# Counts multiplied without stride, tile numbers rounded in floating point, weight halves made ahead of the one-hot loop and in the waits behind it

## The reference

```
xn = layernorm(x)                                   # 4096 tokens of 256
scores = softmax(xn @ gate_w.T + gate_b)            # 8 experts
top_w, top_i = top_k(scores, 2)
y = sum over the two experts: top_w * ((silu(xn @ w1.T + b1) * (xn @ w3.T + b3)) @ w2.T + b2)
z = (silu(xn @ ws1.T + bs1) * (xn @ ws3.T + bs3)) @ ws2.T + bs2
out = x + time_mix(xn) + y + z
```

## Time and profile before

| what | value |
|---|---|
| median of 3 runs | 474.6 (473.55 to 476.1) |
| profiled execution: its own time | 473.8 |
| profiled execution: span from first to last instruction | 472.0 |
| mean granted clock of TensorE | 0.985 of full speed |
| busy: TensorE / VectorE / ScalarE / GpSimd | 440.8 (93%) / 365.9 (78%) / 241.6 (51%) / 230.3 (49%) |
| chain that ended last: TensorE / VectorE / GpSimd / ScalarE | 64% / 14% / 9% / 4% |

### The profile page before, as it was taken

The page is one execution under the profiler, slowest core; times in us unless marked ns, Lnnn a source line. Parts: engine busy times, 40 slices in busy tenths (PEclk is TensorE's granted clock), DMA queues, the critical chain, the costliest instruction groups (busy, mean ns, idle before and its releaser), DMA issues.

```text
span 472.0 us, 8323 instructions
## 1 busy us (share of the span) xinstructions
PE 440.8 (93%) x2534; PEld 370.8 (79%) x2534; DVE 365.9 (78%) x684; ACT 241.6 (51%) x396; POOL 230.3 (49%) x224
## 2 busy tenths in 40 slices
PE   0998687979999999999999899999999999999997
PEld 0562455858888888888888778798888989898987
DVE  5976968968787887878766689995968787877863
ACT  4777734678668595966765532333324132324131
POOL 3333747434858666488854377651433415160000
PEclk9999679999999999999999999999999999999999
DMA  7999923245764865443473773826153443431001
GB/s 228 341 305 395 228 69 101 80 178 190 253 215 146 264 184 167 135 134 117 123 208 109 288 273 97 274 63 214 56 165 115 126 152 123 156 113 67 24 24 44
DMA packets 45858, 77.24 MB, mean 164 GB/s; under 512 B 5908, under 2 KB 32252, under 8 KB 45820
## 3 DMA queue, kind: packets, MB, share of 16 engines
q1 hardware_dynamic: 37580, 55.87, 34.1%
q0 software_dynamic: 8240, 20.88, 17.0%
HBM read 48.52 MB, written 28.21 MB: 163 GB/s over the span
## 4 chain that ended last, share of the span: by engine, by line
PE 64%; DVE 14%; POOL 9%; issue 7%; ACT 4%; DMA 1%; SPq 0%; DVEq 0%; POOLq 0%; ACTq 0%
PE ps_g L1109 11%; PE ps_y L1109 6%; PE ps_w L1569 5%; PE ps_w L1571 5%; PE ps_w L1570 5%; PE ps_w L1635 5%; PE ps_w L1636 5%; PE ps_w L1634 5%; POOL xg L1032 4%; PE ps_G L619 3%; PE ps_x L1103 2%; PE ps_h L1129 2%; PE ps_T L605 2%; PE ps_v L1570 1%; PE ps_r L1571 1%
## 5 line engine op out<-in xcount | busy, mean ns | idle before, releaser
L1032 POOL DMA_INDIRECT xg<-xn_rows,tile_tok x71 | 71.4, 1005 | 26.7 <-issue 18.6
L1545 POOL DMA_INDIRECT yg<-expert_rows,rows x64 | 67.9, 1061 | 23.6 <-issue 17.1
L1109 PE MATMUL ps_g<-w_hi,x_hi 128*128 x142 | 56.2, 396 | 2.2 <-DVE x_lo L1264 2.2
L1109 PE MATMUL ps_g<-w_lo,x_hi 128*128 x142 | 56.3, 396 | 0.0
L1109 PE MATMUL ps_g<-w_hi,x_lo 128*128 x142 | 56.1, 395 | 0.0
L1676 ACT ACTIVATE sact<-ps_w,vec_b 128x512 f32<-128x512 f32 x32 | 22.0, 687 | 58.4 <-PE ps_w L1571 58.4
L1569 PE MATMUL ps_w<-col_hi,s_hi 128*128 128x512 f32 x128 | 50.5, 395 | 0.4 <-DVE shid L1787 0.4
L1570 PE MATMUL ps_w<-col_lo,s_hi 128*128 128x512 f32 x128 | 50.2, 392 | 0.0
L1571 PE MATMUL ps_w<-col_hi,s_lo 128*128 128x512 f32 x128 | 50.2, 392 | 0.0
L1109 PE MATMUL ps_y<-w_hi,h_hi 128*128 x142 | 43.2, 304 | 1.3 <-DVE h_lo L1280 1.3
L1273 DVE TENSOR_TENSOR hid<-ps_g,act 128x512 f32<-128x512 f32 (+1 forms) x36 | 23.7, 659 | 24.4 <-ACT act L1185 24.4
(11 more groups left out here) (255 smaller groups left out, 1276.9 us busy)
## 6 DMA issues: line engine op xcount, KB each, us to landing
expert_rows<-y SPq DMA_DIRECT2D x35, 256.0 KB, 2.2
w_lo<-w_all SPq DMA_DIRECT2D x16, 384.0 KB, 9.9
table<-mix_tables SPq DMA_DIRECT2D x8, 768.0 KB, 6.2
xn_rows<-xn SPq DMA_DIRECT2D x16, 256.0 KB, 8.1
xn_columns<-xT SPq DMA_DIRECT2D x8, 512.0 KB
col<-xn_columns SPq DMA_DIRECT2D x8, 512.0 KB, 5.0
res<-x SPq DMA_DIRECT2D x16, 256.0 KB, 2.9
out<-res SPq DMA_DIRECT2D x16, 256.0 KB, 2.2
```

The costliest lines, as they stand in the source:

```text
L1032: pool.indirect_dma_start(out=xg[b][:, t, :], out_offset=None, in_=xn_d[:, :], in_offset=bass.IndirectOffsetOnAxis(ap=tile_tok[:, first_ti ...
L1109: mm = nc.tensor.matmul(out, x[:, k, :], w[:, ds(e, 1), k, cols].rearrange("p o n -> p (o n)"), start=(k == 0 and n == 0), stop=(last and ...
L1545: pool.indirect_dma_start(out=yg[a.buf(2)][:, k, q, :], out_offset=None, in_=y_d[:, :], in_offset=bass.IndirectOffsetOnAxis(ap=picked[a.bu ...
```

## The change

The counts: `hot` is read as it lies (token block, expert), and the order by expert is made where the result is written into `ps_cnt`. The tile numbers: instead of adding 127, converting to int32, shifting by 7 and converting back, a large constant (128 times 2 to the 23rd) is added and subtracted again in fp32, which rounds to a multiple of 128; `ntile`, `last` and `start` are then in rows and not in tiles, so the product with 128 becomes a sum, and `last_b` is divided by 128 and made behind `start`. ScalarE makes all of `made_hi` and `made_lo` for pieces 0 to 3 before its exponentials, and rounds all 16 pieces before `terms`. TensorE does `rest(2)` and `rest(3)` ahead of the one-hot loop, and loads the registers of the first two duos before `turn_x(0)`. VectorE halves pieces 0 to 3 between `gates` and `terms`, 4 to 7 behind `terms`, and 8 to 11 two by two later.

```
-        MADE, BOTH, HIGH, LOW = 4, 6, 13, 2
+        MADE, BOTH, HIGH, LOW = 4, 6, 16, 8
...
+        WHOLE = float(P << 23)
...
-            for i in range(2):
+            for i in range(MADE):
                 made_hi(act, i)
+            for i in range(MADE):
+                made_lo(act, i)
             nc.scalar.activation(early[:, 0:1], gb[:], ACT.Exp)
             exps(0, 0, EARLY)
             exps(1, EARLY, NSTEP)
...
-            for i in range(2, MADE):
-                made_hi(act, i)
-            for i in range(2):
-                made_lo(act, i)
             act.wait_ge(s_xn, NSTEP)
             act.wait_ge(s_xna, NSTEP)
             for i in range(MADE, HIGH):
                 split(i)
-            for i in range(2, MADE):
-                made_lo(act, i)
             act.wait_ge(s_terms, 3)
...
-                    mm = nc.tensor.matmul(ps_cnt[:, h, :].rearrange("p (e j) -> p e j", e=E), sums[:],
-                                          hot[:, k].rearrange("p j e -> p e j"), start=(k == 0), stop=(k == TOPK - 1))
+                    mm = nc.tensor.matmul(ps_cnt[:, h, :].rearrange("p (e j) -> p j e", e=E), sums[:], hot[:, k],
+                                          start=(k == 0), stop=(k == TOPK - 1))
             mm.then_inc(s_cnt, 1)
             for i in range(FIRST, MADE):
                 less(i)
-            for i in range(FIRST):
+            for i in range(MADE):
                 rest(pe, i)
...
-            for i in range(FIRST, BOTH):
+            for i in range(MADE, BOTH):
                 rest(pe, i)
...
-            own.link(nc.vector.tensor_scalar(ntile_i[:], filled[:, :, NT - 1], float(P - 1), float(P), ALU.add,
-                                             ALU.max))
-            own.link(nc.vector.tensor_scalar(ntile_i[:], ntile_i[:], 7, None, ALU.arith_shift_right))
-            own.link(nc.vector.tensor_copy(ntile[:], ntile_i[:]))
+            own.link(nc.vector.tensor_scalar(ntile[:], filled[:, :, NT - 1], (P - 1) / 2, WHOLE, ALU.add, ALU.add))
+            own.link(nc.vector.tensor_scalar(ntile[:], ntile[:], WHOLE, float(P), ALU.subtract, ALU.max))
             own.link(nc.vector.tensor_tensor_scan(out=last[:], data0=ones_f[:, 0:E], data1=ntile[:],
                                                   initial=0.0, op0=ALU.mult, op1=ALU.add))
-            nc.vector.tensor_copy(last_b[:], last[:])
             own.link(nc.vector.tensor_tensor(start[:], last[:], ntile[:], ALU.subtract))
-            own.link(nc.vector.scalar_tensor_tensor(out=place, in0=start[:, None, :].broadcast_to([P, NT, E]),
-                                                    scalar=float(P), in1=place, op0=ALU.mult, op1=ALU.add))
+            nc.vector.tensor_scalar(last_b[:], last[:], 1.0 / P, None, ALU.mult)
+            own.link(nc.vector.tensor_tensor(place, place, start[:, None, :].broadcast_to([P, NT, E]), ALU.add))
...
             nc.vector.tensor_tensor(gates[:, 1, :], gates[:, 1, :], gates[:, 0, :], ALU.mult)
+            for i in range(4):
+                split_lo(dve, i)
             dve.wait_ge(s_terms, 4)
...
-            for i in range(LOW):
+            for i in range(4, LOW):
                 split_lo(dve, i)
...
-            es = {}
             pe.wait_ge(s_tok, 1)
+            es = {a: experts(a) for a in range(2)}
             turn_x(0)
...
-            for i in range(HIGH, E * KC):
-                split_hi(act, i)
             cut_x(2)
...
-            for i in range(LOW, 5):
-                split_lo(dve, i)
             cut_x(0)
-            for i in range(5, 8):
+            for i in range(8, 10):
                 split_lo(dve, i)
             hidden(0)
             cut_x(1)
-            for i in range(8, 12):
+            for i in range(10, 12):
                 split_lo(dve, i)
```

More of the change, by code:

```diff
@@ L298, in route @@
         eps_t = sb("eps_t", [P, 1], F32)
-        ntile_i = sb("ntile_i", [P, E], I32)
+        WHOLE = float(P << 23)
         ntile = sb("ntile", [P, E], F32)
@@ L806, in vector @@
                                                   data0=keep[:].rearrange("p e j -> p (e j)"),
-                                                  data1=ps_cnt[:, 1, :], initial=0.0,
-                                                  op0=ALU.mult, op1=ALU.add))
+                                                  data1=ps_cnt[:, 1, :], initial=0.0, op0=ALU.mult, op1=ALU.add))
             own.link(nc.vector.tensor_tensor(place.rearrange("p j e -> p e j"), filled[:], prefix, ALU.add))
-            own.link(nc.vector.tensor_scalar(ntile_i[:], filled[:, :, NT - 1], float(P - 1), float(P), ALU.add,
-                                             ALU.max))
-            own.link(nc.vector.tensor_scalar(ntile_i[:], ntile_i[:], 7, None, ALU.arith_shift_right))
-            own.link(nc.vector.tensor_copy(ntile[:], ntile_i[:]))
+            own.link(nc.vector.tensor_scalar(ntile[:], filled[:, :, NT - 1], (P - 1) / 2, WHOLE, ALU.add, ALU.add))
+            own.link(nc.vector.tensor_scalar(ntile[:], ntile[:], WHOLE, float(P), ALU.subtract, ALU.max))
             own.link(nc.vector.tensor_tensor_scan(out=last[:], data0=ones_f[:, 0:E], data1=ntile[:],
                                                   initial=0.0, op0=ALU.mult, op1=ALU.add))
-            nc.vector.tensor_copy(last_b[:], last[:])
             own.link(nc.vector.tensor_tensor(start[:], last[:], ntile[:], ALU.subtract))
-            own.link(nc.vector.scalar_tensor_tensor(out=place, in0=start[:, None, :].broadcast_to([P, NT, E]),
-                                                    scalar=float(P), in1=place, op0=ALU.mult, op1=ALU.add))
+            nc.vector.tensor_scalar(last_b[:], last[:], 1.0 / P, None, ALU.mult)
+            own.link(nc.vector.tensor_tensor(place, place, start[:, None, :].broadcast_to([P, NT, E]), ALU.add))
             own.link(nc.vector.tensor_tensor(prod[:], hot[:], place[:, None].broadcast_to([P, TOPK, NT, E]),
@@ L1151, in tensor @@
                     mm.then_inc(c_turn, 1)
-            es[0] = experts(0)
             up(0, es[0])
             turn_x(1)
-            es[1] = experts(1)
             up(1, es[1])
@@ L1347, in vector @@
             dve.wait_ge(t_carry, 1)
-            for i in range(LOW, 5):
-                split_lo(dve, i)
+            assert LOW == 8
             cut_x(0)
-            for i in range(5, 8):
+            for i in range(8, 10):
                 split_lo(dve, i)
```

## The result

| | kernel before | the change |
|---|---|---|
| median | 474.55 (472.49 to 477.1, 22 runs) | 479.07 (472.38 to 480.73, 22 runs) |
| profiled execution: time / span / mean granted clock | 473.8 / 472.0 / 0.985 | 479.9 / 478.1 / 0.975 |
| busy: TensorE / VectorE / ScalarE / GpSimd | 440.8 / 365.9 / 241.6 / 230.3 | 445.6 / 366.5 / 242.1 / 235.6 |

The ratio is 1.0046 (95% interval 1.0023 to 1.0068); it is smaller than the ratio of the medians, 1.0095, because it leaves out runs more than 1.5% above the fastest of their kernel, and with two of the 22 runs of the change at 472.4 (clock 0.985) that is its slowest third, the profiled execution included. The other 20 lie between 476.3 and 480.7 at a clock of 0.971 to 0.978, and the profiled one, at 479.9, is 0.8 above the median. The forecast was 471.8.

A forecast was written before the change was run, and what follows sets the result against it. TensorE's matmuls bound the kernel from `up(0)` at 71.06 on, so only its start counts. VectorE's `x_lo(0)` moving from 70.40 to 67.6 gains 2.8: 473.8 - 2.8 = 471.0, as median 471.8, range 470.8 to 474.4 without the clock rival.

The forecast's parts named there:

- the part on ScalarE: ScalarE's weight halves ahead of `terms`: last gathered subtraction lands at 62.0, halves end at 63.5, VectorE's `terms` starts at 64.25.
- The clock rival: With two rests behind the loop, half clock lasts through three `up`s, costing 7.1 against 2.8: 478.9; chance 0.12.
- The gathers: Ahead of `x_hi(0)`: the first gather starts at 64.28 - 1.1 and lands 3.0 later, at 66.2.
- S: How much earlier VectorE is from the four terms ahead of the one-hot loop: 1.1, from -0.3 to 1.8.
- (a): Ahead of the loop: the four count matmuls read `hot` without stride, gaining 0.9, at most 1.31.
- The rival of the dear write: The counts' strided write into `ps_cnt` costs as much as the strided read or twice that: 472.6 to 474.4; chance 0.17.
- (b): Ahead of the loop on VectorE: one linked operation of the tile count goes, gaining 0.21.
- (c): Ahead of the loop on VectorE: `last_b` moves behind `start`, gaining 0.2 of 0.28, lower bound 0.
- (d): `rest(2)` and `rest(3)` ahead of the loop on TensorE end at 50.07; cost 0.2, bounds 0 and 0.55.
- The gathers bind: GpSimd's gathers start only 1.1 earlier while the expert loop runs 2.8 earlier; if one is late, 473.5; chance 0.16.

The follow-up runs named there:

- gap_high14: The change with a 64-column memset ending each one-hot loop pass and weight halves 14 and 15 put back behind `up(0)` on ScalarE: 470.94, ratio 0.9887.
- gap_reduce: The change with halves 14 and 15 put back, memsets in passes 1 to 3, row sum and reciprocal of `share` in passes 5 and 6: 471.03, ratio 0.9894.
- order_only: The change's order of work on ScalarE, TensorE and VectorE, with counts and tile numbers of the kernel before: 476.44, ratio 1.0039.
- counts_only: The kernel before with only the change's counts and tile numbers: 473.60, ratio 0.9974.
- warm: The change with 14 unread matmuls added on TensorE, ten ahead of `turn_x(0)` and four ahead of `up(0)`: 475.55, ratio 0.9988.
- high13: The change with weight halves 13 to 15 put back behind `cut_x(1)` on ScalarE: 472.32, ratio 0.9917.
- gap_two: The change with a 64-column addition of two SBUF inputs at the end of each one-hot loop pass: 480.02, ratio 1.0113.

## Why the prediction was wrong, point by point

**The step that failed** is in the part on ScalarE: "Taking 62.0 for that landing, halves 14 and 15 end at 63.5". It carried GpSimd's times over from the trace of before, as if GpSimd's instructions depended only on their data. The halves could start at 67.52, 5.5 later than that; `up(0)` came at 73.69 and not at 68.3, 5.4 later. This one term is the whole error in `up(0)`: what lies behind it was right, with 73.69 - 69.74 = 3.95 from VectorE's `terms` to `up(0)` for a forecast of 68.3 - 64.25 = 4.05. The span came out 8.9 longer than forecast (6.1 lost for 2.8 gained): these 5.4, and 3.5 of clock, which the forecast had left to a rival.

**The clock rival** was given 0.12 and the price 478.9. The time agrees by luck, the mechanism only in part. Its premise, that two rests might not suffice, was wrong, and the argument against it right: full clock came back at 66 after two rests. What it left out is what follows: I had TensorE go on at 66.2, and it stood until 69.09. Half clock then lasted through nearly two `up`s and cost 3.54, not 7.1 over three; a lateness of 2.63, where that rival still had the gain of 2.8, more than made up for the difference.

**The gathers** were held to start S behind the old time, at 63.2. They started at 65.88, not because `tile_tok` was late but because GpSimd's queue was. That queue was followed only forward from `tile_tok`, not backward to what GpSimd still had to do.

**What was right.** (a) The counts took 41.99 to 43.03, 1.04 against 1.97: 0.93 for a forecast of 0.9, about 0.2 each. The rival of the dear write falls: written at a stride, a count matmul takes less than half of the 0.445 that it took when read at a stride. The Trainium skill (Advanced Engine Details and Errata, PSUM Cachelines) says that a non-contiguous pattern in PSUM slows matmuls significantly. Against 0.117, worked out for contiguous columns, a price does remain in these 0.2; but the prediction's reading of that sentence, that the counts would gain nothing or lose, is refuted by the 0.93. S came out as 1.24 for 1.1, but partly by another route. VectorE's timeline of the kernel before:

```profile
43.67 0.69 DVE L805 TENSOR_TENSOR_SCAN map<-keep,ps_T 128x256 f32<-128x256 f32 x1 [2.06 <-PE ps_T L663]
...
46.84 0.69 DVE L822 TENSOR_TENSOR prod<-hot,map 128x512 f32<-128x512 bf16 x1
...
49.22 0.46 DVE L837 TENSOR_TENSOR hot_tile<-part_b,lane_b 128x568 f16<-128x568 f16 x1
...
57.28 1.79 DVE L850 CAST tile_exp<-exp_f 128x71 int32<-128x71 f32 x1
...
60.51 0.69 DVE L853 TENSOR_TENSOR xin<-part_b,lane_b 128x1024 f16<-128x1024 f16 x1 [0.39 <-PE ps_T L675]
...
63.26 0.20 DVE L865 TENSOR_SCALAR tile_tok<-tok_f 128x71 int32<-128x71 f32 x1
```

and the same steps of the change:

```profile
43.07 0.69 DVE L801 TENSOR_TENSOR_SCAN map<-keep,ps_T 128x256 f32<-128x256 f32 x1 [1.13 <-PE ps_T L659]
...
45.96 0.69 DVE L814 TENSOR_TENSOR prod<-hot,map 128x512 f32<-128x512 bf16 x1
...
48.55 0.46 DVE L829 TENSOR_TENSOR hot_tile<-part_b,lane_b 128x568 f16<-128x568 f16 x1
...
56.52 0.19 DVE L842 CAST tile_exp<-exp_f 128x71 int32<-128x71 f32 x1
```

(b) and (c) gave 3.17 - 2.89 = 0.28 (scan to product) for a forecast of 0.41. The loop starts only 0.67 earlier, as the counts themselves began 0.33 later (41.99 against 41.66). The other 0.57 arose inside the loop. In the kernel before, the conversion L850 took 1.79, to 59.07, where it takes 0.19 in the change; TensorE's next batch started only at 59.24, and in the last pass VectorE waited 0.39 for its buffer (L853 at 60.51). In the change it doesn't wait. The hold of L850 falls together with a memset of GpSimd:

```profile
57.47 1.54 POOL L509 MEMSET terms<- 128x1024 f32 x1
```

That GpSimd held VectorE there fits this, but no run tests it.

(d) The rests ended at 50.35 (forecast 50.07) and the loop hid them. The two rests behind the loop ended at 66.08 (forecast 66.1). And gap_high14 and gap_reduce show that the idea of the forecast was sound where halves 14 and 15 don't stand ahead of `terms` and the standstill is cured: `up(0)` came at 69.48 and 68.75 at full clock, 1.6 and 2.3 earlier than before, if not 2.8. TensorE waits for the first gather in both (0.54 and 0.44), which is the prediction's rival *The gathers bind*, at `up(0)`.

**What stays open.** GpSimd got in at some ends of two-input operations (its first L394 in the loop took 1.55) and not at others, and the memsets change that without standing at those ends; no run tells what decides. The two runs of the change at 472.4 weren't profiled: that they had no standstill is only likely.

## What to carry to other kernels

A time read for one engine holds only while its neighbours keep their rhythm: where GpSimd issues transfers beside a dense run of two-input VectorE operations, its times can't be carried over, and nothing that the path needs should stand behind the last of them in anybody's queue. In such a loop a memset in every pass is worth a try; here eight of 0.09 were worth 6 us. A row sum or a reciprocal let GpSimd in as well, but an operation with one input isn't enough in general: the conversion of 0.2 stood inside the hold in four profiles and didn't end it. And whoever takes filler work from TensorE should ask what happens to the clock if the next input comes some us late.

## What the runs showed of the hardware

- A GpSimd instruction that issues gathered transfers, 1.54 alone, took 2.79 to 6.22 beside back-to-back two-input VectorE operations, and ended 1.41 or 1.42 after the last of them ahead of a row sum or a reciprocal, eleven times in seven profiles (the change, order_only, counts_only, warm, high13, gap_two, gap_reduce). A memset each pass cured it, an addition didn't. The Trainium skill (SBUF — State Buffer, Who interferes with whom) says that a VectorE instruction with two SBUF inputs contends with a GpSimd instruction that reads SBUF, and a `tensor_reduce` never does: the runs agree. It infers, however, that `tensor_tensor` leaves the issuing of transfers alone; here the whole instruction that issues them was held, be it in reading its indices or in issuing, which no run separates.
- The other way round, VectorE's conversions were long beside a memset of GpSimd. The one of L850, 0.19 in the change, took 1.79 in the kernel before and ended at 59.07, as GpSimd's memset L509 ended (57.47 to 59.01); in gap_high14 it took 2.15 and ended at 59.01, again with that memset's end (58.96). In order_only the conversion to `tile_tok`, 0.20 in the change, took 1.08 to 64.62, with the memset from 63.03 to 64.57. Three coincidences in three profiles, and no run made to test them.
- Full clock, just granted at 66, was lost again after TensorE had stood from 66.08 to 69.09, and half clock then lasted from about 69.5 to 83. With 14 matmuls more in that stretch (warm) it stayed full.
